# Self attention, two cross attentions and one maximum: three stages of a post-layernorm decoder, re-ordered

## The chip, the cores and the metric

The kernel runs on one core of one Trainium2 chip. A core has a matrix engine (TensorE, PE in the rows), a vector engine (VectorE, DVE), an activation engine (ScalarE, ACT) and a general one (GpSimd, POOL); SyncE (SP) issues the transfers here. The engines run at the same time and keep order through semaphores that the program sets and waits for. The metric is the time of the device for one launch, in microseconds, as the median of several runs.

## The reference

`x` is [32, 56, 128] (32 sequences of 56 tokens, width 128), `ctx` is [32, 1500, 128]. Six sublayers follow each other, each inside `x = layernorm(x + sublayer(x))`. The ones that the change touches are the first, the second and the fifth.

```python
def _L0_attn_ref(x, ...):            # 16 heads of 8, window of 32
    scores = einsum('bhqd,bhkd->bhqk', q, k) * scale + sliding_window_bias(S)
    attn = softmax(scores); out = einsum('bhqk,bhkd->bhqd', attn, v)
    return out.reshape(B, S, D) @ wo.T + bo
def _L0_xattn_ref(k, v, q, ...):     # one head of 128, k = v = ctx
    qp = q @ Wq.T + bq; kp = k @ Wk.T; vp = v @ Wv.T + bv
    return (softmax(qp @ kp.T * scale) @ vp) @ Wo.T + bo
def _L1_xattn_ref(x, context, ...):  # 16 heads of 64, 1500 keys
    q = (_layernorm(x, ln_gamma, ln_beta) @ w_q); k, v = split(context @ w_kv)
    attn = softmax(einsum('bqhd,bkhd->bhqk', q * SCALE, k))
    return (einsum('bhqk,bkhd->bqhd', attn, v) @ w_out + b_out) * tanh(gate)
```

The others are a mixture of experts (top 2 of 8, exact gelu) as the third, a gated state-space layer as the fourth, and a mixture of experts with a shared one (silu) as the sixth.

## The kernel before

Two sequences make a pair: 128 rows on the partitions, 64 for each with 56 in use. There are 16 pairs. Tokens stay on the chip between sublayers, once with rows on the partitions (`x_tok`) and once turned (`x_feat`). Each sublayer is a phase with a block of its own: a program for each engine, written by hand. The order within an engine is the order of the code, and the semaphores between engines are all that ties them.

**PairSteps** drives the first two phases. A step runs every stage once, each on another pair: in self attention project (lag 0), scores 1, transpose 2, attend 3, output 4, norm 5, so six pairs are under way. Each engine's `step(i, s)` asks `pair(i, s, "scores")` and so on for its pair and issues what that stage has for the engine. The body of the loop holds two steps; steps ahead of it fill and steps behind it drain. **Tail** ends each sublayer: VectorE takes the moments of the row sum `r` (L261, L265), GpSimd makes `rstd` of them (L270, L275), VectorE normalises to `xn` (L292), GpSimd copies it to `x_tok`, TensorE turns it, ScalarE stores it in `x_feat` (L349), and where a router follows TensorE makes 8 logits and VectorE copies them (L359).

**Self attention** (`self_attention_phase`, prefix `sa_`). GpSimd expands the keys of a pair so that each head has its own columns (`kexp`, L469, two instructions of 128x896) and adds the output bias to the tokens of a pair (`xbo`). TensorE makes the scores (L510). VectorE adds the window mask (L583, `sm`), takes the maximum of each head (L588), subtracts it (L590), sums after ScalarE's exponential (L597, L599), keeps the masked values (`vexp`, L603), adds projected output and `xbo` (L612, `r`), and keeps the attended values divided by the sum (`on`, L622). The output projection is L549; the attended values stand behind it.

**First cross attention** (`context_attention_phase`, prefix `ca_`). Stages: project 0, scores 1, transpose 2, values 3, output 4, norm 5. Scores fill four banks of PSUM with 375 columns each; one VectorE instruction takes the negated maximum over the 1500 (L907). The probabilities are turned by TensorE (12 blocks, in three parts of four) and copied by VectorE and ScalarE (L915, L939). VectorE also takes the greatest magnitude of the context, one reduction over 128x3000 a step (`ca_tops`, L946), which the second cross attention needs; the next load of `ctxT` into this buffer (L728, on SyncE's queue) waits for it and for the scores. `qp` (L901) is the projected query with bias and scale, L922 makes `r`.

**Second cross attention** (`cross_attention_phase`, prefix `xa_`). The queries of a pair are multiplied ahead with the product of key and query weights (L2072), so the context itself is the key. A pair has 14 units, 7 for each sequence; a unit is 8 queries times 16 heads on 128 rows against 1500 keys, in three banks of 500 columns. Units take banks 0 to 2 and 3 to 5 in turn. For precision queries and context are split in a high and a low part, so TensorE makes three matmuls for each bank: L2087, L2088, L2089. Then, for a unit:

- VectorE takes the maximum in two instructions: L2215 over the first two banks, into a spare column (500) of the second bank; L2219 over that second bank's whole 512 columns from there on, which are that column, eleven filled with a very low number, and the third bank's 500.
- ScalarE takes the exponential over the three banks with its sum (L2333); VectorE sums up and inverts (L2224, L2226).
- ScalarE writes the high part of the probabilities to SBUF (L2349), VectorE the low part, piece by piece (L2234, three instructions). Each of these frees one bank (`h2_ready`) for the unit after the next.
- The probabilities are turned by a transposing DMA, in two units of a pair by TensorE with copies by VectorE (L2240). The matmuls on values (L2112 to L2114) come per group of units.

In a step VectorE's order is: inverse of the unit before, turned copy if any, maximum of this unit, the low part of the unit before. In slots 2 to 5 TensorE also projects (L2072) for the next pair; in slots 7 to 9 it makes the output of the pair before; in 10 to 13 stand the residual, normalise, store and logits of that pair.

## Time and profile before

| what | us |
|---|---|
| median of 3 runs (lowest, highest) | 2001.07 (1999.9, 2002.27) |
| profiled execution: its time, its span | 1998.59, 1996.9 |
| TensorE busy: matmuls, weight loads | 1750.6 (88%), 1266.5 (63%) |
| VectorE, ScalarE, GpSimd busy | 1593.3 (80%), 1186.7 (59%), 830.3 (42%) |
| masked additions L583 of self attention, 16 | starts 28.8 to 141.2 |
| context loads L728 of the first cross attention | issued 181.5 to 317.2 |
| score matmuls L2087 of the second cross attention, 672 | starts 701.6 to 1776.4 |

Durations and stretches come from one profiled execution. The three stages can be told apart in it by their lines. The second cross attention takes more than half of the span, some 1080 us of 1997; each of the other two takes between 110 and 190. Busy shares over the span mix the stages, so a table by stretches is more use.

### The profile page before, as it was taken

To read this page: it belongs to the slowest core of one execution; us is meant where nothing else is said; L and a number is where in the kernel's file an instruction comes from. 1 tells how busy PE (TensorE), PEld (TensorE's weight loads), DVE (VectorE), ACT (ScalarE), POOL (GpSimd) and SP (SyncE) were. 2 spreads that over 40 slices of the span, in tenths; PEclk is the share of its full clock that TensorE was granted. 3 is DMA by queue.
4 is the path that set the end of the run, shared out by engine and by line. 5 is a ranking of instruction groups with operands and counts; after the bars stand their busy time and mean duration, and the time that the engine had idled before them with its cause. 6 is when DMAs were issued, how large, how long until landed. Compare 5 with 4: busy or idle time off the path is not lost. (4 is left out here: it accounts for less than half of the span.)

```text
span 1996.9 us, 34496 instructions
## 1 busy us (share of the span) xinstructions
PE 1750.6 (88%) x10381; PEld 1266.5 (63%) x10381; DVE 1593.3 (80%) x2986; ACT 1186.7 (59%) x1868; POOL 830.3 (42%) x705
## 2 busy tenths in 40 slices
PE   4886888699956379999999999999999999994997
PEld 3554656688842256666667666766666676654886
DVE  3884676678867379988998999899889988966887
ACT  2441332577732167777777777777777777754553
POOL 4660111223342373636364545455454546322333
PEclk9997998699976589999999999999999999997998
DMA  5101775100000079898989888989888998971000
GB/s 192 77 0 62 301 279 233 43 1 0 1 0 0 32 157 206 174 192 178 193 175 192 184 189 178 186 186 182 188 179 191 179 196 173 190 127 72 6 5 10
DMA packets 623534, 264.97 MB, mean 133 GB/s; under 512 B 601565, under 2 KB 605693, under 8 KB 622717
## 3 DMA queue, kind: packets, MB, share of 16 engines
q1 hardware_dynamic: 623468, 264.19, 57.1%
q8 instruction: 31, 0.51, 0.1%
q14 instruction: 35, 0.28, 0.0%
HBM read 112.24 MB, written 0.92 MB: 57 GB/s over the span
## 5 line engine op out<-in xcount | busy, mean ns | idle before, releaser
L2234 DVE SCALAR_TENSOR_TENSOR xa_h<-xa_psum,xa_rinv,xa_h 128x500 f16<-128x500 f32 x672 | 452.5, 729 | 0.7 <-ACT xa_h L2349 0.7
L2333 ACT ACTIVATE xa_psum<-xa_psum,xa_negmax 128x1500 f32<-128x1500 f32 x224 | 332.7, 1485 | 198.0 <-DVE xa_negmax L2219 198.0
L2349 ACT ACTIVATE xa_h<-xa_psum,xa_rinv 128x1000 f16<-128x1000 f32 x448 | 372.2, 883 | 82.5 <-DVE xa_rinv L2226 81.2
L2215 DVE TENSOR_REDUCE xa_psum<-xa_psum 128x1 f32<-128x1000 f32 x224 | 269.5, 1203 | 88.1 <-PE xa_psum L2089 88.1
L2087 PE MATMUL xa_psum<-xa_c_hi,xa_q_hi 128*128 128x500 f32 x672 | 282.9, 421 | 28.5 <-DVE xa_h L2234 18.3
L2112 PE MATMUL xa_psum<-xa_prT,xa_n_hi 128*128 128x512 f16 (+1 forms) x768 | 272.9, 355 | 2.4 <-DMA xa_prT<-xa_h 1.5
L2114 PE MATMUL xa_psum<-xa_prT,xa_n_lo 128*128 128x512 f16 (+1 forms) x768 | 270.7, 352 | 0.0
L2113 PE MATMUL xa_psum<-xa_prT,xa_n_hi 128*128 128x512 f16 (+1 forms) x768 | 270.7, 352 | 0.0
L2088 PE MATMUL xa_psum<-xa_c_lo,xa_q_hi 128*128 128x500 f32 x672 | 262.5, 391 | 0.0
L2089 PE MATMUL xa_psum<-xa_c_hi,xa_q_lo 128*128 128x500 f32 x672 | 262.2, 390 | 0.0
L2219 DVE TENSOR_REDUCE xa_negmax<-xa_psum 128x1 f32<-128x512 f32 x224 | 154.9, 691 | 25.8
L2006 POOL CAST xa_q_hi<-xa_q_full 128x896 fp32r<-128x896 f32 x32 | 29.9, 934 | 347.5 <-PE xa_psum L2089 336.5
L2087 PEld LDWEIGHTS xa_psum<-xa_c_hi,xa_q_hi 128*128 128x128 f32 x672 | 127.4, 190 | 71.9 <-DVE xa_h L2234 31.7
L1406 DVE TENSOR_TENSOR moe_hid_lo<-moe_hid,moe_hid_hi 128x448 fp32r<-128x448 f32 x200 | 127.5, 667 | 31.3 <-ACT moe_hid_hi L1542 26.0
L2089 PEld LDWEIGHTS xa_psum<-xa_c_hi,xa_q_lo 128*128 128x128 f32 x672 | 127.2, 189 | 26.1
L2112 PEld LDWEIGHTS xa_psum<-xa_prT,xa_n_hi 128*128 128x128 f16 x768 | 76.0, 99 | 104.4 <-issue 55.0
L2026 POOL TENSOR_SCALAR xa_ctxP<-xa_ctxP,xa_n_scale 128x1536 f32<-128x1536 f32 x32 | 133.3, 4167 | 17.5 <-DMA xa_ctxP<-in_ctxP 17.5
L2088 PEld LDWEIGHTS xa_psum<-xa_c_lo,xa_q_hi 128*128 128x128 f32 x672 | 128.1, 191 | 11.5
L2114 PEld LDWEIGHTS xa_psum<-xa_prT,xa_n_lo 128*128 128x128 f16 x768 | 75.1, 98 | 70.1
L1253 POOL TENSOR_TENSOR moe_acc<-moe_acc,moe_part 128x448 f32<-128x448 f32 x52 | 63.5, 1222 | 123.2 <-DVE moe_part L1459 65.6
L1538 ACT ACTIVATE moe_hid<-moe_psum,up_bias 128x448 f32<-128x448 f32 x128 | 83.9, 656 | 43.9 <-PE moe_psum L1294 40.0
L2019 POOL TENSOR_TENSOR xa_c_lo<-xa_ctxT,xa_c_hi 128x1500 fp32r<-128x1500 f32 x32 | 107.9, 3372 | 2.6
(303 smaller groups left out, 3613.8 us busy)
## 6 DMA issues: line engine op xcount, KB each, us to landing
ctxN<-in_ctxP SPq DMA_DIRECT2D x16, 1536.0 KB, 9.2
xa_ctxP<-in_ctxP SPq DMA_DIRECT2D x32, 768.0 KB, 4.4
ctxT<-in_ctxT SPq DMA_DIRECT2D x16, 1500.0 KB, 6.3
xa_ctxT<-in_ctxT SPq DMA_DIRECT2D x32, 750.0 KB, 4.9
xa_prT<-xa_h SPq DMA_TRANSPOSE x192, 5.5
up<-in_F_up SPq DMA_DIRECT2D x1, 2048.0 KB, 9.2
down<-in_F_down SPq DMA_DIRECT2D x1, 2048.0 KB, 13.3
gate<-in_F_gate SPq DMA_DIRECT2D x1, 1024.0 KB, 4.8
```

The costliest lines, as they stand in the source:

```text
L2026: pool.tensor_scalar(ctxP[:, :], ctxP[:, :], n_scale[:, :], None, ALU.mult).then_inc(n_scaled, 1)
L2087: nc.tensor.matmul(out, qh, c_hi[:, b, a:z], start=True, stop=False)
L2088: nc.tensor.matmul(out, qh, c_lo[:, b, a:z], start=False, stop=False)
L2089: done = nc.tensor.matmul(out, ql, c_hi[:, b, a:z], start=False, stop=True)
L2112: nc.tensor.matmul(out, nh, ph, start=(kt == 0), stop=False)
L2113: nc.tensor.matmul(out, nh, pl, start=False, stop=False)
L2114: done = nc.tensor.matmul(out, nl, ph, start=False, stop=(kt == KT - 1))
L2215: nc.vector.tensor_reduce(psum[:, bank + 1, W:W + 1], psum[:, bank:bank + 2, 0:W], AX.XY, ALU.max)\
L2219: nc.vector.tensor_reduce(negmax[:, s % 2, :], flat_psum[:, top:top + 512], AX.X, ALU.max, negate=True)\
L2234: nc.vector.scalar_tensor_tensor(h[:, H_SLOT[s], 1, a:z], psum[:, bank + j, 0:W], rinv[:, s % 2, :], h[:, H_SLOT[s], 0, a:z], ALU.mult, AL ...
L2333: nc.scalar.activation(psum[:, bank:bank + 3, 0:W], psum[:, bank:bank + 3, 0:W], ACT.Exp, bias=negmax[:, s % 2, :], accum_out=rs[:, s % 2, ...
L2349: nc.scalar.activation(h[:, H_SLOT[s], 0, a * W:z * W].rearrange("p (a c) -> p a c", c=W), psum[:, bank + a:bank + z, 0:W], ACT.Identity, ...
```

## The change

It has three parts. In **self attention** the bias row is added to all of `x_tok` once at the start, by VectorE, in place of GpSimd's addition for each pair. VectorE sums and inverts ahead of the normalise; the subtraction (L613 of the kernel after) stands behind the masked values, no longer right behind the maximum. GpSimd expands keys ahead of its store. TensorE's turned output and output projection come later in the step, the attended values are cut in two parts around the turned `xn`, and scores go half by half of the heads. ScalarE keeps `oT` later.

In the **first cross attention** the reduction over the context is cut in two (one for each sequence), the first behind the negated maximum, the second at the end of the step; `top_ready` counts halves. `qp` comes ahead of the normalise, the logits have a stage of their own (lag 6), values come in three parts, and TensorE's transposes come ahead of the turned output.

In the **second cross attention** a unit's maximum is one instruction over its three banks, behind all nine matmuls; the spare column, its filling and the semaphore between the two instructions go.

```diff
--- before.py
+++ after.py
@@ -412,7 +412,6 @@
...
-                at = pair(i, s, "attend")
-                if at:
-                    j, p = at
-
-                    pool.wait_ge(t.r_ready, last(j, p + 1, PER))
-                    pool.tensor_tensor(xbo[:, p:p + 1, :], k.x_tok[:, bass.ds(j * PER + p, 1), :],
-                                       k.bo_row0[:, :].unsqueeze(1), ALU.add).then_inc(xbo_ready, 1)
+                at = pair(i, s, "norm")
+                if at:
+                    t.pool_store(pool, *at)
...
+            def attend(j, p, part):
+
+                if part == 0:
+                    pe.wait_ge(prT_kept, this(j, p + 1, PER))
+                    pe.wait_ge(v_kept, this(j, p + 1, PER))
+
+                    pe.wait_ge(o_kept, this(j, p, PER))
+                for hp in range(part * HP // 2, (part + 1) * HP // 2):
+                    for half in range(2):
+                        done = nc.tensor.matmul(psum[half * SP:(half + 1) * SP, 6, hp * 16:(hp + 1) * 16],
+                                                prT[:, p, hp, half * SP:(half + 1) * SP],
+                                                vexp[:, p, half, hp * 16:(hp + 1) * 16], start=True, stop=True)
+                if part:
+                    done.then_inc(o_ready, 1)
+
...
+                at = pair(i, s, "output")
+                if at:
+                    j, p = at
+                    pe.wait_ge(o_kept, this(j, p + 1, PER))
+
+                    pe.wait_ge(t.r_ready, this(j, p, PER))
+                    nc.tensor.transpose(psum[:, 7, 0:128], on[:, p, :], k.ident[:, :]).then_inc(oT_ready, 1)
+                at = pair(i, s, "attend")
+                if at:
+                    attend(*at, 0)
...
+            nc.vector.tensor_tensor(k.x_tok[:, :, :], k.x_tok[:, :, :],
+                                    k.bo_row0[:, :].unsqueeze(1).to_broadcast([128, PAIRS, D]), ALU.add).then_inc(rows_biased, 1)
+            dve.wait_ge(rows_biased, 1)
 
...
-                    dve.wait_ge(xbo_ready, this(j, p + 1, PER))
-                    nc.vector.tensor_tensor(t.r[:, p, :], psum[:, 7, 128:256], xbo[:, p, :], ALU.add)\
-                        .then_inc(t.r_ready, 1)
+                    nc.vector.tensor_tensor(t.r[:, p:p + 1, :], psum[:, 7, 128:256].unsqueeze(1),
+                                            k.x_tok[:, bass.ds(j * PER + p, 1), :], ALU.add).then_inc(t.r_ready, 1)
                     t.vector_moments(dve, j, p)
...
-    steps = PairSteps(project=0, scores=1, transpose=2, values=3, output=4, norm=5)
+    steps = PairSteps(project=0, scores=1, transpose=2, values=3, output=4, norm=5, logits=6)
...
+                sp.sem_inc(issuing, 1)
+                sp.wait_ge(top_ready, last(i, 2 * p + 2, 2 * PER))
...
-                for kt in range(part * KT // 2, (part + 1) * KT // 2):
+                for kt in range(part * KT // 3, (part + 1) * KT // 3):
...
-                    pe.wait_ge(t.logits_kept, n(i, s, 6))
...
+                at = pair(i, s, "logits")
+                if at:
+                    pe.wait_ge(qp_kept, n(i, s, 0))
+                    pe.wait_ge(t.r_ready, n(i, s, 5))
+                    pe.wait_ge(t.feat_stored, n(i, s, 6))
+                    t.tensor_logits(pe, *at, psum[:, 7, 384:384 + E])
...
+                at = pair(i, s, "values")
+                if at:
+                    j, p = at
...
-                    pe.wait_ge(qp_kept, n(i, s, 0))
+                    pe.wait_ge(t.logits_kept, n(i, s, 6))
...
+                    values(at[1], 1)
...
-                    values(at[1], 1).then_inc(pv_ready, 1)
+                    values(at[1], 2).then_inc(pv_ready, 1)
...
-                at = pair(i, s, "norm")
-                if at:
-                    pe.wait_ge(t.feat_stored, n(i, s, 5))
-                    pe.wait_ge(t.r_ready, n(i, s, 4))
-                    pe.wait_ge(qk_kept, n(i, s, 0))
-                    t.tensor_logits(pe, *at, psum[:, 7, 384:384 + E])
...
+            def top(i, s, half):
+
+                at = pair(i, s, "scores")
+                if at:
+                    j, p = at
+                    if half == 0:
+                        dve.wait_ge(ctxT_loaded[p], (j + 1) * 16)
+                    nc.vector.tensor_reduce(tops[:, bass.ds(j * 2 * PER + 2 * p + half, 1)], ctxT[:, p, half, :], AX.X,
+                                            ALU.max, apply_absolute_value=True).then_inc(top_ready, 1)
+
             def step(i, s):
...
+                top(i, s, 0)
...
-                    dve.wait_ge(ctxT_loaded[p], (j + 1) * 16)
-                    nc.vector.tensor_reduce(tops[:, bass.ds(j * PER + p, 1)], ctxT[:, p, :, :], AX.XY, ALU.max,
-                                            apply_absolute_value=True).then_inc(top_ready, 1)
+                top(i, s, 1)
...
+                at = pair(i, s, "project")
+                if at:
...
-                    if j:
-                        done.then_inc(scores_ready, 1)
+                done.then_inc(scores_ready, 1)
...
             def maximum(i, s):
                 bank = 3 * (s % 2)
-                top = (bank + 1) * 512 + W
-                dve.wait_ge(scores_ready, this(i, 2 * s + 1, 2 * NU))
-                nc.vector.tensor_reduce(psum[:, bank + 1, W:W + 1], psum[:, bank:bank + 2, 0:W], AX.XY, ALU.max)\
-                    .then_inc(two_ready, 1)
-                dve.wait_ge(two_ready, this(i, s + 1, NU))
-                dve.wait_ge(scores_ready, this(i, 2 * s + 2, 2 * NU))
-                nc.vector.tensor_reduce(negmax[:, s % 2, :], flat_psum[:, top:top + 512], AX.X, ALU.max, negate=True)\
+                dve.wait_ge(scores_ready, this(i, s + 1, NU))
+                nc.vector.tensor_reduce(negmax[:, s % 2, :], psum[:, bank:bank + 3, 0:W], AX.XY, ALU.max, negate=True)\
                     .then_inc(max_ready, 1)
 
```

VectorE in self attention, one step of the filling: `sa_sm` are the scores, `sa_mx` their maxima, `sa_rs` and `sa_rinv` sum and inverse, `sa_r` the row sum. Before:

```order
L292 TENSOR_SCALAR sa_xn<-sa_r,sa_mean_var,sa_rstd 128x128
L583 TENSOR_TENSOR sa_sm<-sa_psum,window_mask 128x896
L588 TENSOR_REDUCE sa_mx<-sa_sm 128x16
L590 TENSOR_TENSOR sa_sm<-sa_sm,sa_mx 128x896
L597 TENSOR_REDUCE sa_rs<-sa_pr 128x16
L599 RECIPROCAL sa_rinv<-sa_rs 128x16
L603 TENSOR_TENSOR sa_vexp<-sa_psum,value_mask 112x256
L612 TENSOR_TENSOR sa_r<-sa_psum,sa_xbo 128x128
L261 BN_STATS sa_moments<-sa_r 128x6
L265 BN_AGGR sa_mean_var<-sa_moments 128x2
L622 TENSOR_TENSOR sa_on<-sa_psum,sa_rinv 128x128
```

and after:

```order
L581 TENSOR_REDUCE sa_rs<-sa_pr 128x16
L583 RECIPROCAL sa_rinv<-sa_rs 128x16
L292 TENSOR_SCALAR sa_xn<-sa_r,sa_mean_var,sa_rstd 128x128
L593 TENSOR_TENSOR sa_sm<-sa_psum,window_mask 128x896
L598 TENSOR_REDUCE sa_mx<-sa_sm 128x16
L605 TENSOR_TENSOR sa_vexp<-sa_psum,value_mask 112x256
L613 TENSOR_TENSOR sa_sm<-sa_sm,sa_mx 128x896
L620 TENSOR_TENSOR sa_r<-sa_psum,x_tok 128x128
L261 BN_STATS sa_moments<-sa_r 128x6
L265 BN_AGGR sa_mean_var<-sa_moments 128x2
L630 TENSOR_TENSOR sa_on<-sa_psum,sa_rinv 128x128
```

Sum and reciprocal moved from behind the subtraction to the head of the step, and the subtraction (L590, now L613) past the masked values.

VectorE in the first cross attention, one step: `ca_tops` is the reduction over the context, `ca_qp` the projected query. Before:

```order
L292 TENSOR_SCALAR ca_xn<-ca_r,ca_mean_var,ca_rstd 128x128
L901 TENSOR_SCALAR ca_qp<-ca_psum,bq0x 128x112
L907 TENSOR_REDUCE ca_negmax<-ca_psum 128x1
L915 COPY ca_prT<-ca_psum 128x512
L922 SCALAR_TENSOR_TENSOR ca_r<-ca_psum,ca_rinv,ca_xb 128x128
L261 BN_STATS ca_moments<-ca_r 128x6
L265 BN_AGGR ca_mean_var<-ca_moments 128x2
L931 RECIPROCAL ca_rinv<-ca_rs 128x1
L359 COPY logits<-ca_psum 128x8
L939 COPY ca_prT<-ca_psum 128x512
L946 TENSOR_REDUCE ca_tops<-ctxT 128x1
```

and after, with the last reduction of the step before in the first row (in the loop the logits copy stands behind L292):

```order
L910 TENSOR_REDUCE ca_tops<-ctxT 128x1
L920 TENSOR_SCALAR ca_qp<-ca_psum,bq0x 128x112
L292 TENSOR_SCALAR ca_xn<-ca_r,ca_mean_var,ca_rstd 128x128
L934 COPY ca_prT<-ca_psum 128x512
L940 TENSOR_REDUCE ca_negmax<-ca_psum 128x1
L910 TENSOR_REDUCE ca_tops<-ctxT 128x1
L948 SCALAR_TENSOR_TENSOR ca_r<-ca_psum,ca_rinv,ca_xb 128x128
L261 BN_STATS ca_moments<-ca_r 128x6
L265 BN_AGGR ca_mean_var<-ca_moments 128x2
L957 RECIPROCAL ca_rinv<-ca_rs 128x1
L959 COPY ca_prT<-ca_psum 128x512
L910 TENSOR_REDUCE ca_tops<-ctxT 128x1
```

The copy of the turned probabilities now comes ahead of the negated maximum, and the reduction (L946, now L910) stands twice, once between the negated maximum and `ca_r` and once at the end.

VectorE in the second cross attention, from the turned copy of one unit to its low part. Before:

```order
L2239 REGISTER_ALU
L2240 COPY xa_prT<-xa_psum 128x4x2x128
L2214 REGISTER_ALU
L2215 TENSOR_REDUCE xa_psum<-xa_psum 128x1
L2217 REGISTER_ALU
L2218 REGISTER_ALU
L2219 TENSOR_REDUCE xa_negmax<-xa_psum 128x1
L2234 SCALAR_TENSOR_TENSOR xa_h<-xa_psum,xa_rinv,xa_h 128x500 x3
```

and after:

```order
L2244 REGISTER_ALU
L2245 COPY xa_prT<-xa_psum 128x4x2x128
L2223 REGISTER_ALU
L2224 TENSOR_REDUCE xa_negmax<-xa_psum 128x1
L2238 REGISTER_ALU
L2239 SCALAR_TENSOR_TENSOR xa_h<-xa_psum,xa_rinv,xa_h 128x500 x2
L2238 REGISTER_ALU
L2239 SCALAR_TENSOR_TENSOR xa_h<-xa_psum,xa_rinv,xa_h 128x500
```

One reduction stands where two stood; nothing else changed places.

## Rows read from the trace of the kernel before

**Rows 1.** Stretches: us, busy of PE (count), PEld, DVE, ACT, POOL; PEclk, DMA, GB/s

```profile
46.67:141.22 94.55, 80.88 (x723) 57.32 (x724) 77.12 (x133) 39.96 (x83) 65.13 (x71) 0.93 0.13 55
216.88:313.80 96.92, 81.25 (x775) 56.81 (x774) 68.57 (x101) 28.15 (x72) 13.24 (x37) 1.00 0.75 291
766.80:1716.30 949.50, 939.76 (x5391) 650.50 (x5391) 855.83 (x1527) 709.78 (x981) 482.57 (x253) 1.00 0.89 185
```

**Rows 2.** Self attention, VectorE in time: start us, us, work [wait]; then L590's durations

```profile
93.85 0.35 DVE L292 TENSOR_SCALAR sa_xn<-sa_r,sa_mean_var,sa_rstd 128x128 f32<-128x128 f32 x1 [0.85 <-POOL sa_rstd L275]
...
100.96 0.34 DVE L292 TENSOR_SCALAR sa_xn<-sa_r,sa_mean_var,sa_rstd 128x128 f32<-128x128 f32 x1 [0.72 <-POOL sa_rstd L275]
...
L590 DVE TENSOR_TENSOR sa_sm<-sa_sm,sa_mx x16: 1091/1235/2637, 31.1 to 143.5; 128x896 f32<-128x896 f32 x16
```

**Rows 3.** Self attention, TensorE and GpSimd in time

```profile
89.09 0.46 PE L549 MATMUL sa_psum<-woT,sa_oT 128*128 128x128 f32 x2 [0.81 <-ACT x_feat L349]
...
101.80 3.34 POOL L469 TENSOR_TENSOR sa_kexp<-sa_kf,head_mask 128x896 f32<-128x896 f32 x2
```

**Rows 4.** First cross attention, around the turn of one step, in time

```profile
259.90 3.27 DVE L946 TENSOR_REDUCE ca_tops<-ctxT 128x3000 f32 x1
...
263.43 0.37 SPq L728 DMA_DIRECT2D ctxT<-in_ctxT  x1
...
263.58 1.71 DVE L907 TENSOR_REDUCE ca_negmax<-ca_psum 128x1 f32<-128x1500 f32 x1
...
263.72 0.33 PE L825 MATMUL ca_psum<-ident,ca_o_tok 128*128 128x128 f32 x1 [1.06 <-DVE ca_qp L901]
...
265.21 0.68 DVE L915 COPY ca_prT<-ca_psum 128x512 f32<-128x512 f32 x1
...
268.33 0.49 PE L867 MATMUL ca_psum<-value_out,ca_oT 128*128 128x128 f32 x2
...
268.86 0.35 DVE L922 SCALAR_TENSOR_TENSOR ca_r<-ca_psum,ca_rinv,ca_xb 128x128 f32<-128x128 f32 x1 [2.97 <-PE ca_psum L867]
...
270.42 0.47 PE L805 MATMUL ca_psum<-x_feat,wqT0x 128*128 x2 [0.75 <-DVE logits L359]
```

**Rows 5.** Second cross attention, one unit of the first pair, in time

```profile
725.09 0.49 PE L2087 MATMUL xa_psum<-xa_c_hi,xa_q_hi 128*128 128x500 f32 x1 [1.11 <-DVE xa_h L2234]
...
726.56 0.39 PE L2087 MATMUL xa_psum<-xa_c_hi,xa_q_hi 128*128 128x500 f32 x1
...
726.76 1.21 DVE L2215 TENSOR_REDUCE xa_psum<-xa_psum 128x1 f32<-128x1000 f32 x1 [0.17 <-PE xa_psum L2089]
...
727.24 1.04 PE L2072 MATMUL xa_psum<-x_feat,key_query 128*128 128x112 f32 x8
...
728.61 2.02 DVE L2234 SCALAR_TENSOR_TENSOR xa_h<-xa_psum,xa_rinv,xa_h 128x500 f16<-128x500 f32 x3
...
729.39 0.49 PE L2087 MATMUL xa_psum<-xa_c_hi,xa_q_hi 128*128 128x500 f32 x1 [1.11 <-DVE xa_h L2234]
```

**Rows 6.** The same phase, a steady pair: first score matmuls of five units

```profile
1195.91 0.48 PE L2087 MATMUL xa_psum<-xa_c_hi,xa_q_hi 128*128 128x500 f32 x1
...
1200.82 0.48 PE L2087 MATMUL xa_psum<-xa_c_hi,xa_q_hi 128*128 128x500 f32 x1
...
1205.33 0.47 PE L2087 MATMUL xa_psum<-xa_c_hi,xa_q_hi 128*128 128x500 f32 x1
...
1210.65 0.48 PE L2087 MATMUL xa_psum<-xa_c_hi,xa_q_hi 128*128 128x500 f32 x1
...
1215.76 0.47 PE L2087 MATMUL xa_psum<-xa_c_hi,xa_q_hi 128*128 128x500 f32 x1
```

**Rows 7.** The page's groups: busy, mean ns; idle before them, releaser

```profile
L2087 PE MATMUL xa_psum<-xa_c_hi,xa_q_hi 128*128 128x500 f32 x672 | 282.9, 421 | 28.5 <-DVE xa_h L2234 18.3
...
L2219 DVE TENSOR_REDUCE xa_negmax<-xa_psum 128x1 f32<-128x512 f32 x224 | 154.9, 691 | 25.8
```

**Rows 8.** Loads of the turned context (L728), from issue to landing

```profile
DMA to landing us min/median/max: 6.0/6.2/7.7
```

More of the change, by code:

```diff
@@ L507, in step @@
                     pe.wait_ge(masked, this(j, p, PER))
-                    for half in range(2):
-                        for hh in range(2):
+                    for hh in range(2):
+                        for half in range(2):
                             done = nc.tensor.matmul(psum[half * SP:(half + 1) * SP, hh, 0:8 * S], qs[:, p, half, :],
@@ L542, in step @@
                     t.tensor_transpose(pe, *at, psum[:, 7, 256:384])
+                at = pair(i, s, "attend")
+                if at:
+                    attend(*at, 1)
                 at = pair(i, s, "output")
@@ L550, in step @@
                         .then_inc(y_ready, 1)
-                at = pair(i, s, "attend")
-                if at:
-                    j, p = at
-                    pe.wait_ge(prT_kept, this(j, p + 1, PER))
-                    pe.wait_ge(v_kept, this(j, p + 1, PER))
-                    pe.wait_ge(o_kept, this(j, p, PER))
-                    for half in range(2):
-                        for hp in range(HP):
-                            done = nc.tensor.matmul(psum[half * SP:(half + 1) * SP, 6, hp * 16:(hp + 1) * 16],
-                                                    prT[:, p, hp, half * SP:(half + 1) * SP],
-                                                    vexp[:, p, half, hp * 16:(hp + 1) * 16], start=True, stop=True)
-                    done.then_inc(o_ready, 1)
             steps.run(pe, step)
@@ L670, in step @@
                                          psum[0:2 * S, 4:6, :], ACT.Copy).then_inc(prT_kept, 1)
+                at = pair(i, s, "output")
+                if at:
+                    j, p = at
+                    act.wait_ge(oT_ready, this(j, p + 1, PER))
+                    act.wait_ge(y_ready, last(j, p + 1, PER))
+                    nc.scalar.activation(oT[:, p, :], psum[:, 7, 0:128], ACT.Identity, bias=k.bv0[:, :])\
+                        .then_inc(oT_kept, 1)
                 at = pair(i, s, "norm")
@@ L916, in step @@
                         .then_inc(even_kept, 1)
+                at = pair(i, s, "scores")
+                if at:
+                    j, p = at
+                    dve.wait_ge(scores_ready, this(j, p + 1, PER))
+                    nc.vector.tensor_reduce(negmax[:, p, :], psum[:, 0:4, 0:Q4], AX.XY, ALU.max, negate=True)\
+                        .then_inc(max_ready, 1)
+                top(i, s, 0)
                 at = pair(i, s, "output")
@@ L940, in step @@
                         .then_inc(even_kept, 1)
[L941 to L947 removed]
+                top(i, s, 1)
             steps.run(dve, step)
[L950 removed]
+            dve.wait_ge(top_ready, last(PAIRS // PER, 2 * PER, 2 * PER))
             nc.vector.tensor_reduce(k.ctx_max[:, :], tops[:, :], AX.X, ALU.max).then_inc(ctx_max_ready, 1)
```

123 lines of the change are left out of this document (47 added, 76 removed).

## The prediction

> **What bounds the kernel now.** The change touches three stages, so I read the table of stretches first [rows 1]. Self attention, between the masked additions of the fourth and the sixteenth pair, runs 12 steps in 94.55 us, 7.88 each. The first cross attention runs 9 steps in 96.92 us, 10.77 each. The second cross attention runs 14 pairs of 14 units in 949.5 us: 67.82 a pair, 4.84 a unit. TensorE is busy 86%, 84% and 99%, VectorE 82%, 71% and 90%. Busy shares don't say who waits for whom, so I then read each stage in order of time.
>
> Self attention: from one normalise to the next 7.11 us pass on VectorE, 0.72 of them waiting for the rstd of GpSimd [rows 2], since normalise stands first in the step and the moments it needs were made just before. VectorE's own work is thus 6.39. TensorE idles 0.81 of the same step before the output projection, which waits for x_feat [rows 3]: 6.30. Some steps are longer than 7.1: the subtraction takes 1.09 us at the least and 2.64 at the most [rows 2] while GpSimd works 3.34 of each step on the expanded keys [rows 3].
>
> First cross attention: the reduction over the context (3.27 us) is the last VectorE instruction of a step; behind it stand normalise and qp, and TensorE waits 1.06 us for qp before its transposition. It waits 0.75 more, at the start of a step, for the logits copy [rows 4]. So TensorE needs 10.77 - 1.06 - 0.75 = 8.96 us.
>
> Second cross attention: TensorE does the nine score matmuls of a unit, then values and what else the unit has. The next unit's scores wait for VectorE's low part, which frees their banks, and which stands behind the maximum. This loop is seen bare in the first pair [rows 5]: scores at 725.09, first maximum at 726.76 (after six matmuls, +1.67), low part at 728.61 (+1.85), next scores at 729.39 (+0.78): 4.30 us, with TensorE idle for 1.11. In the steady pairs TensorE has 4.91 of work in a unit with a projection, 5.32 and 5.11 with outputs, 4.51 with a turn [rows 6]. So this loop is hidden nearly everywhere, but by 0.2 to 0.6 us only.
>
> **The second cross attention after.** VectorE now issues one reduction of 128x1500 where it issued 1000 and 512. The same shape is in the first cross attention: 1.71 us, and the next instruction starts 1.63 after its start [rows 4]. Against the 1.85 of the two, VectorE saves 0.22 a unit. But the reduction can't start after six matmuls any more. Nine are issued in 2.15 us, and the last three of them in 0.68 (726.56 to 727.24) [rows 5], so it starts at +1.67 + 0.68 = +2.35. The loop becomes 2.35 + 1.63 + 0.78 = 4.76, and 0.46 longer where it was bare.
>
> What lies beside other work: the four projection units (4.91) and the three output units (5.32, 5.11 and, not shown, as much again) stay TensorE's, 35.2 us. The other seven units of a pair took 67.82 - 35.2 = 32.6, and take 7 x 4.76 = 33.3 after, plus 0.07 for the unit where the logits copy stands between maximum and low part: +0.8 a pair, +11 for 14 pairs. In the first pair thirteen units run on the bare loop or near it, and in the last pair, where projections are missing, seven do: about 20 x 0.35 = +7. Sum: +18. ScalarE, the transposes by DMA and GpSimd have slack: the exponential moves 0.4 later, and the high part waits for it, but the low part that reads it is a maximum further on. Bounds for the unknown, the reduction's length: from 1.71 (its row) up to 1.90, the two old durations together (1.21 and 0.69) [rows 7]; that gives a loop of 4.95 and +35. Down: if part of the third group's wait were hidden, 4.60, about +5.
>
> **The first cross attention after.** On VectorE qp now stands first, normalise second, the logits copy third, the reduction is cut in two halves, one behind the negated maximum (where VectorE waited for the output matmul) and one at the end; logits are a stage later, so TensorE no longer ends its step on them. Each half is about 1.7 (a 128x1500 row). Both waits go. What is late next: (a) the new step's first matmul needs r: the output matmul starts at 268.33 and r at 268.86 [rows 4], r lasts 0.35, so 1.1 us lie between the output matmul and the next step, of which TensorE fills, as I count, 1.0 with the last four transposes; (b) logits, now right behind the scores, need qp, and qp waits for the second half reduction, which ends some 2.8 us into the step, while scores end at 2.9: about 0.3 of wait. 8.96 + 0.3 = 9.25 a step. From the fifth step to the sixteenth's scores 11 steps gain 1.5: -16.5; filling is bound by context loads, issued only behind a reduction as before, and draining sheds 1.6 of the reduction once: -1. Sum -17. Bounds: 8.96 and no wait, -21; context loads, below, -12.
>
> **Self attention after.** Sum and reciprocal now stand ahead of normalise, 1.3 us of work that covers the 0.72; the output projection stands behind attend, which covers the 0.81; the bias row is added once for all pairs, so GpSimd loses an addition a step. Neither engine waits then, and VectorE's 6.39 is the longer one: 6.45 with TensorE beside it. 12 x (7.88 - 6.45) = -17. Filling and draining: the sum now waits for the whole exponential, which nothing covers before outputs exist, an estimated +1 (it works on as many elements as the subtraction, 1.09), and the single addition over 128x2048 runs before any key is expanded, about 2.3 us (1.09 for 896) in a time when VectorE had nothing to do, and may hold GpSimd's first keys back, +0.5. Drain steps lose an attend's wait, -1. Sum -16.5. The reordering inside scores and attend I take at 0; it cannot cost more than the idle it leaves.
>
> **A rule weighed.** The subtraction is not slower by a steady factor; it is 1.09 or up to one key expansion longer [rows 2]. The Trainium skill, SBUF, "Who interferes with whom", says that a VectorE instruction with two SBUF inputs and a GpSimd instruction that reads SBUF shut each other out for a whole instruction. The trace agrees, with 2.64 against 1.09. By that rule the new placement matters: the keys of a step end, by my count, 0.05 us before the later subtraction starts. If it starts first, 1.5 us a step can be lost again; that is the third rival.
>
> **Sum.** +18 - 17 - 16.5 = -15.5 against the profiled execution: span 1996.9, its time 1998.6. That is 1983. The median of the runs shown, 2001.1, lies 2.5 above this execution, so I predict 1985.5.
>
> **The rivals.**
> First: VectorE bounds the second cross attention, and a shorter maximum is a plain gain. For it: busy 90%, the tightest of the three stages, in which TensorE's score matmuls waited 18.3 us for the low part [rows 7]. The Trainium skill, VectorE: DVE Perf Modes, section on the TRN2 errata, says that each instruction pays a fixed cost and that few large ones are better. By rows: all these waits of TensorE go, 18.3 us, and in total 2001 - 33 - 18 = 1950. Against it: VectorE is idle before the maximum in the bare loop and TensorE waits all the same [rows 5]. Chance 0.05.
> Second, slower: the bare loop grows past 4.91. Then the four projection units pay as well, eleven a pair, and each further 0.1 costs 1.1 x 14 + 2 = 17 us. The gains of 33.5 are eaten when the loop reaches about 4.93, that is when the reduction lasts 1.88, not 1.71. At 2.0 it is 5.05 and the total about 2018. For it: three banks of 500 in one instruction were never timed here; against it: the 1.71 row spans four banks. Chance 0.07.
> Third: subtraction and key expansion meet in every second step, self attention keeps 7.1 or so: -8 in place of -16.5, total 1994. Chance 0.13.
> Fourth: context loads bind the first cross attention. A load lands 6.0 to 7.7 us after its issue [rows 8], which is 0.26 behind the reduction's end [rows 4]; at a step of 9.25 about 6.5 us are left for it. If loads take 7.5, steps are 9.7: 5 us less gain, 1990. Chance 0.12.
> Fifth: the reordering changes neither stage much because each wait removed is replaced by a neighbour's, 2003 with the second cross attention's +18 and half the gains. Chance 0.05.
>
> **Numbers.** Forecast 1977 to 1993, chance 0.58. The range that holds 8 in 10 goes from 1972 (all small bounds good) to 1998, where rivals three and four together end. A measurement of this kernel tells 0.2%, 4 us, from nothing. Faster: forecast, first, fourth, most of the third: 0.85. Same, 1997 to 2005: 0.08. Slower: 0.07.
>
> **What would show it.** In the second cross attention a reduction of 1.71, the bare loop at 4.76, pairs at 68.6, TensorE's idle before the first score matmul up, VectorE's busy time down. In the first, steps of 9.25 and no wait for qp before the transposition. In self attention steps of 6.45, a normalise without wait, subtractions of 1.09. Wrong would be: pairs under 67.8 or over 70, steps over 10 or over 7.

## The result, and the profile after

| | before | after |
|---|---|---|
| median, us (lowest, highest; runs) | 2002.12 (1999.9, 2006.05; 8) | 1992.47 (1988.81, 1996.72; 8) |
| profiled execution's span | 1996.9 | 1988.5 |
| VectorE busy | 1593.3 | 1568.3 |

The ratio is 0.9948, with a 95% interval from 0.9934 to 0.9961: 10.4 us less, between 7.8 and 13.2. The forecast was 15.5 less. Faster, clear of the noise though only by half a percent, and two thirds of the size. The median of 1992.47 lies inside the range of 1977 to 1993 by half a microsecond only.

I compare when the same events start in the two traces:

| event | before | after | difference |
|---|---|---|---|
| 4th masked addition, self attention | 46.67 | 46.77 | +0.1 |
| 16th masked addition | 141.22 | 129.96 | -11.3 |
| 1st negated maximum, first cross attention | 176.47 | 162.26 | -14.2 |
| 16th negated maximum | 327.82 | 301.04 | -26.8 |
| first score matmul, second cross attention | 701.6 | 670.6 | -31.0 |
| last of them | 1776.4 | 1767.6 | -8.8 |

So some 31 us were won before the second cross attention began, and 22 were given back in it. The table of stretches of the kernel after (us, busy of PE, PEld, DVE, ACT, POOL, PEclk, DMA share, GB/s) answers to [rows 1]; the stretches run between the same events, but the last holds fourteen pairs within 1 us:

```profile
46.77:129.96 83.19, 68.39 (x719) 46.55 (x717) 78.98 (x133) 38.57 (x82) 50.06 (x59) 1.00 0.15 63
207.20:291.91 84.71, 82.15 (x778) 56.00 (x776) 69.99 (x109) 28.76 (x73) 12.98 (x36) 1.00 0.86 331
758.00:1718.60 960.60, 949.87 (x5379) 648.71 (x5378) 829.41 (x1330) 707.65 (x978) 481.79 (x252) 1.00 0.88 183
```

Self attention's twelve steps take 6.93 each (7.88 before), nine steps of the first cross attention 9.41 (10.77), a pair of the second 68.61 (67.82). In self attention VectorE is now busy 95%, and TensorE's granted clock is 1.00 where it was 0.93 (1.00 is 2.4 GHz, and it falls to 0.50, 1.2 GHz, for some us at a time).

**Self attention.** One step in order of time, VectorE and GpSimd, which answers to [rows 2, 3]:

```profile
86.48 1.08 DVE L581 TENSOR_REDUCE sa_rs<-sa_pr 128x16 f32<-128x896 f32 x1
...
87.06 3.33 POOL L465 TENSOR_TENSOR sa_kexp<-sa_kf,head_mask 128x896 f32<-128x896 f32 x2
...
87.88 0.95 DVE L292 TENSOR_SCALAR sa_xn<-sa_r,sa_mean_var,sa_rstd 128x128 f32<-128x128 f32 x1
...
88.75 1.08 DVE L593 TENSOR_TENSOR sa_sm<-sa_psum,window_mask 128x896 f32<-128x896 f32 x1
```

The durations (lowest, median, highest, in ns) of the normalise and the subtraction:

```profile
L292 DVE TENSOR_SCALAR sa_xn<-sa_r,sa_mean_var,sa_rstd x16: 288/954/1200, 52.5 to 151.5; 128x128 f32<-128x128 f32 x16
...
L613 DVE TENSOR_TENSOR sa_sm<-sa_sm,sa_mx x16: 1081/1082/1091, 31.8 to 132.4; 128x896 f32<-128x896 f32 x16
```

VectorE doesn't wait for the rstd in front of the normalise any more, as forecast, and the subtraction is at its 1.08. But the normalise, 0.35 before, has a median of 0.95; in the steady steps it is 0.95 and 1.14 in turn. The masked addition behind it starts at 88.75: that is 87.06 plus 1.69, the end of the first of GpSimd's two key instructions.

**First cross attention.** Around the turn of a step, answering to [rows 4]:

```profile
249.68 0.47 PE L814 MATMUL ca_psum<-x_feat,wqT0x 128*128 x2 [0.23 <-DVE ca_r L948]
...
250.72 1.70 DVE L910 TENSOR_REDUCE ca_tops<-ctxT 128x1500 f32 x1
252.34 0.32 DVE L920 TENSOR_SCALAR ca_qp<-ca_psum,bq0x 128x112 f32<-128x112 f32 x1
...
252.67 0.37 SPq L739 DMA_DIRECT2D ctxT<-in_ctxT  x1
252.75 0.39 PE L355 MATMUL ca_psum<-router,ca_xnT 128*128 128x8 f32 x2
...
259.28 2.75 PE L825 MATMUL ca_psum<-ctxT,ca_qk 128*64 128x375 f32 x16
```

TensorE doesn't wait for qp here, where it waited 1.06, and it waits 0.23 for `ca_r` ahead of the projection, where it waited 0.75 for the logits copy. The next load is issued 0.25 behind the end of the second half (250.72 plus 1.70).

**Second cross attention.** One unit of the first pair, answering to [rows 5]:

```profile
696.89 0.49 PE L2098 MATMUL xa_psum<-xa_c_hi,xa_q_hi 128*128 128x500 f32 x1 [1.58 <-DVE xa_h L2239]
...
699.05 1.04 PE L2083 MATMUL xa_psum<-x_feat,key_query 128*128 128x112 f32 x8
699.25 1.72 DVE L2224 TENSOR_REDUCE xa_negmax<-xa_psum 128x1 f32<-128x1500 f32 x1 [0.86 <-PE xa_psum L2100]
...
701.54 1.37 DVE L2239 SCALAR_TENSOR_TENSOR xa_h<-xa_psum,xa_rinv,xa_h 128x500 f16<-128x500 f32 x2
701.67 0.50 PE L2098 MATMUL xa_psum<-xa_c_hi,xa_q_hi 128*128 128x500 f32 x1 [1.58 <-DVE xa_h L2239]
```

The reduction lasts 1.72, it starts 2.36 after the first score matmul, and the unit takes 4.78. VectorE has less work and waits more; TensorE waits 1.58 where it waited 1.11.

### The profile page after: what moved, and what is told of

It is laid out like the page before. It is cut to its first block and busy times, and to the rows that moved or that the text cites. A ratio compares the mean times of both kernels' runs of the same rounds, so it can differ in the third digit from the quotient of the medians.

```text
span 1988.5 us, 34045 instructions
## 1 busy us (share of the span) xinstructions
PE 1749.0 (88%) x10381; PEld 1249.8 (63%) x10381; DVE 1568.3 (79%) x2777; ACT 1184.4 (60%) x1868; POOL 810.5 (41%) x689
## 5 line engine op out<-in xcount | busy, mean ns | idle before, releaser
L2224 DVE TENSOR_REDUCE xa_negmax<-xa_psum 128x1 f32<-128x1500 f32 x224 | 385.5, 1721 | 166.9 <-PE xa_psum L2100 166.9
L2122 PEld LDWEIGHTS xa_psum<-xa_prT,xa_n_hi 128*128 128x128 f16 x768 | 76.0, 99 | 104.4 <-issue 55.1
L2123 PEld LDWEIGHTS xa_psum<-xa_prT,xa_n_hi 128*128 128x128 f16 x768 | 75.6, 98 | 49.1
```

The source lines that it names most:

```text
L2122: nc.tensor.matmul(out, nh, ph, start=(kt == 0), stop=False)
L2123: nc.tensor.matmul(out, nh, pl, start=False, stop=False)
L2224: nc.vector.tensor_reduce(negmax[:, s % 2, :], psum[:, bank:bank + 3, 0:W], AX.XY, ALU.max, negate=True)\
```

## The experiments

Unless said otherwise a run's kernel is timed against the kernel before on the same chip; a difference in us is the ratio's times 2001. Intervals are 95%.

**The three parts, one at a time.** The kernels take whole functions from one kernel or the other, so no edit is shown.

> The kernel before with the single maximum of the second cross attention and nothing else of the change. Theory (the loop scores, maximum, low part, next scores has become 4.76 us, and only units in which TensorE has less than that pay): +21.6 us as read from the starts of the maxima in the trace after (6.6 in the first pair, 12.0 in fourteen steady pairs, 3.0 in the last), so about 2023 in place of 2001, a maximum of 1.72 us and a bare loop of 4.76. Rival (part of the 21.6 is due to the stages ahead, which end earlier in another state of clock or queues): 10 to 17 us.

Measured: 2021.08, ratio 1.0104 (1.0085 to 1.0123), +20.8 us. Bare units are 4.75 to 4.79. The theory stands; the 17 of the rival lies at the edge of the interval (17.0 to 24.6), but in this run's profile the stage alone, from its first maximum to its last, is 1093.2 where it was 1072.0, so 21.2 of it are the stage's own.

> The kernel after with the maximum of before in two instructions: both reorderings without the new maximum. Theory: the gains of the two stages stand by themselves, -30 us against before (1971), and the bare loop is 4.30 again. Rival (the earlier stages' gain is partly given back in the second cross attention whatever its maximum, since the first loads and the first clock dip move with it): only -20 to -25.

Measured: 1967.70, ratio 0.9847 (0.9825 to 0.9869), -30.6. Bare units are 4.30. The rival falls.

> The kernel before with the new order of self attention alone. Theory: -14 us (to 1987): steady steps of 7.03 in place of 7.87, the drain 3 shorter, the start 0.7 longer. Rival (part of the shorter drain and the early start of the first cross attention belongs to that phase's own new order): -11, as far as the last masked addition shows.

Measured: 1985.65, ratio 0.9926 (0.9908 to 0.9945), -14.8. The theory's size; the rival's -11 lies at the edge of the interval.

> The kernel before with the new order of the first cross attention alone. Theory: -15.5 (to 1985.5): steady steps of 9.38 in place of 10.74, eleven of them 14.7, the drain 3 less, the filling 1.8 to 2 longer since its steps wait for loads of the turned context. Rival (the loads wait only because self attention ends earlier and the context is not yet there): the filling is no longer than before and the gain is -17 to -18.

Measured: 1985.26, ratio 0.9931 (0.9911 to 0.9952), -13.8. Theory and rival both lie in the interval (-17.8 to -9.6). The first five maxima are 10.38, 7.47, 8.60 and 8.54 apart, against 6.77, 7.27, 8.97 and 10.65 before: 1.3 longer. But this filling differs from one execution to the next without any edit: with the order of before it takes 33.7 in the profile of the kernel before and 37.7 in that of the run with the new maximum alone, and with the new order 33.8, 35.4 and 36.3 in three profiles of kernels that are the same up to there (both orders with the maximum of before, the kernel after, the late start below). So the profiles can't tell whether the new order fills more slowly, and theory and rival both stay open.

The three add up to -7.8, the whole is -10.4, within the intervals the same. Parts that touch separate stages add up here.

**Why the new maximum costs.** VectorE's work of before, but with the start of after:

```diff
-                dve.wait_ge(scores_ready, this(i, 2 * s + 1, 2 * NU))
+                dve.wait_ge(scores_ready, this(i, 2 * s + 2, 2 * NU))
```

> Both reorderings with the maximum of before in two instructions, but the first of them waits for all nine matmuls too, as the single maximum does. Theory (the loop's length is what counts, and the late start, not the length of the reduction, is the price): loop 2.35 + 1.85 + 0.78 = 4.98; seven units of a steady pair at 4.98 in place of 32.6 us together give 2.3, the four projection units 0.07 each 0.3, so 36 for fourteen pairs, and 0.68 on 20 bare units 13.6: about +50 over 1967.7, 2018. Rival (VectorE's work sets these units): its work is the same as before, so no more than +5.

Measured: 2027.48, one run, +60 over the run with both orders and the maximum of before (2002 was the kernel before there, 2000 beside that run, so 2 us of it may be the chip's), where +50 was expected. In the profiles 53 of the 60 are in this stage: from its first maximum to its last 1125.8 pass where 1072.4 did. The bare units:

```profile
695.57 1.21 DVE L2229 TENSOR_REDUCE xa_psum<-xa_psum 128x1 f32<-128x1000 f32 x1 [0.84 <-PE xa_psum L2103]
696.82 0.69 DVE L2233 TENSOR_REDUCE xa_negmax<-xa_psum 128x1 f32<-128x512 f32 x1
697.42 2.02 DVE L2248 SCALAR_TENSOR_TENSOR xa_h<-xa_psum,xa_rinv,xa_h 128x500 f16<-128x500 f32 x3
...
698.21 0.50 PE L2101 MATMUL xa_psum<-xa_c_hi,xa_q_hi 128*128 128x500 f32 x1 [1.79 <-DVE xa_h L2248]
...
700.55 1.21 DVE L2229 TENSOR_REDUCE xa_psum<-xa_psum 128x1 f32<-128x1000 f32 x1 [0.85 <-PE xa_psum L2103]
```

From 695.57 to 700.55 is 4.98, as worked out. With no more work for VectorE the kernel loses far more than the change did: the start behind all nine matmuls is the price, and the single instruction gives back 0.22 of its 0.68. The rival falls.

**Why the normalise is three times as long.** First GpSimd's instructions are halved:

```diff
                     for half in range(2):
-                        done = pool.tensor_tensor(kexp[:, p, half, :, :],
-                                                  kf[:, p, half, :].unsqueeze(1).to_broadcast([128, H0, S]),
+                        for a in range(0, H0, H0 // 2):
+                            done = pool.tensor_tensor(kexp[:, p, half, a:a + H0 // 2, :],
+                                                      kf[:, p, half, :].unsqueeze(1).to_broadcast([128, H0 // 2, S]),
...
```

> Both reorderings with the maximum of before (as in the run of both orders without the new maximum, 1967.7), and GpSimd's key expansion in four instructions of 128x448 in place of two of 128x896. Theory A (VectorE's normalise has to wait until the GpSimd instruction that is running ends, for its whole length): the instruction that is in the way is half as long, so the normalise falls from a median of 0.95 to 0.34 to 0.8, the self attention steps from 7.03 to 6.4 to 6.9, the whole 2 to 6 us less. Rival B (the normalise is longer because it waits for something else, such as a semaphore of the turned xn or the rstd): 0.95 stays and the step is 7.03 or, by the fixed cost of two more GpSimd instructions, longer.

Measured: 1965.84, ratio 0.9813 (0.9792 to 0.9834). The durations of the normalise and of the keys, and then three stretches of 20 us (columns as above):

```profile
L292 DVE TENSOR_SCALAR sa_xn<-sa_r,sa_mean_var,sa_rstd x16: 289/390/1101, 52.9 to 146.5; 128x128 f32<-128x128 f32 x16
...
L465 POOL TENSOR_TENSOR sa_kexp<-sa_kf,head_mask x64: 931/936/1154, 22.4 to 122.0; 128x448 f32<-128x448 f32 x64
```

```profile
60.00:80.00 20.00, 18.57 (x178) 11.99 (x176) 18.88 (x34) 9.53 (x22) 15.46 (x22) 0.91 0.01 2
80.00:100.00 20.00, 17.98 (x173) 11.56 (x172) 18.83 (x33) 9.15 (x21) 15.46 (x22) 0.91 0.00 0
100.00:120.00 20.00, 18.75 (x183) 12.19 (x182) 18.91 (x34) 9.78 (x21) 13.80 (x21) 0.91 0.00 0
```

The normalise falls to a median of 0.39 and B falls. But the steps now alternate, 6.28 and 7.28, and the median hides that the normalise does so too: 0.39 in the short steps, 1.07 to 1.10 in the long ones. TensorE's clock, 1.00 in these stretches of the kernel after, is 0.91. In a long step (in order of time) the scores, 1.72 at full clock, take 2.90, and the normalise is 1.10:

```profile
96.03 2.90 PE L518 MATMUL sa_psum<-sa_kexp,sa_qs 128*64 128x448 f32 x8
...
99.37 1.10 DVE L292 TENSOR_SCALAR sa_xn<-sa_r,sa_mean_var,sa_rstd 128x128 f32<-128x128 f32 x1
```

The clock doesn't make the long steps, though. The step from 79.55 on takes 7.27 as well, with its scores at full clock and the stretched normalise:

```profile
82.83 1.72 PE L518 MATMUL sa_psum<-sa_kexp,sa_qs 128*64 128x448 f32 x8
...
85.81 1.09 DVE L292 TENSOR_SCALAR sa_xn<-sa_r,sa_mean_var,sa_rstd 128x128 f32<-128x128 f32 x1
```

This normalise starts 0.1 before the first key instruction ends (84.99 plus 0.94) and lasts to the end of the second, so halving the instruction shortens the wait in every second step only. The twelve steps save 3.9 us. The total is not clearly below that of the run without this edit.

The second run moves GpSimd's store ahead of its keys, so that keys can't start before the normalise has ended:

```diff
             def step(i, s):
+                at = pair(i, s, "norm")
+                if at:
+                    t.pool_store(pool, *at)
                 at = pair(i, s, "project")
```

> Both reorderings with the maximum of before, but GpSimd does its store (which waits for the normalise) ahead of the key expansion, as in the kernel before. Theory A (the two engines shut each other out for whole instructions): the normalise is back at 0.34, but the keys now run over the subtraction, which has two inputs in SBUF: it rises from 1.08 to between 1.6 and 2.6 in most steps, and the steps are 7.0 or longer, up to 7.9. Rival B (the normalise waits for something of its own): it keeps about 0.95 and the subtraction 1.08.

Measured: 1974.34, one run. Most steps are 7.6 to 7.8, the mean is 7.5.

```profile
L292 DVE TENSOR_SCALAR sa_xn<-sa_r,sa_mean_var,sa_rstd x16: 289/346/348, 52.3 to 155.2; 128x128 f32<-128x128 f32 x16
...
L613 DVE TENSOR_TENSOR sa_sm<-sa_sm,sa_mx x16: 1081/2376/2432, 31.6 to 138.7; 128x896 f32<-128x896 f32 x16
```

The normalise is never over 0.35, and the subtraction has taken its place with a median of 2.38. A holds in both directions: what meets a key instruction waits for its end, and the order only chooses which. The two wait differently: the normalise ends with the key instruction, the subtraction 0.94 behind it (85.26 plus 2.41 is 87.67, the key instruction ends at 86.73).

The third takes the normalise from VectorE:

```diff
+                    nc.scalar.activation(t.xn[:, p, :], t.r[:, p, :], ACT.Identity, bias=minus_mean[:, p, :],
+                                         scale=t.rstd[:, p, :]).then_inc(t.xn_ready, 1)
...
-                    t.vector_normalise(dve, *at)
```

> Both reorderings with the maximum of before, and self attention's normalise on ScalarE as scale and bias (GpSimd makes -mean x rstd in two more small instructions). VectorE then has no instruction left that a key expansion meets, and 0.34 less work. Theory A: VectorE's step is 7.03 - 0.95 = 6.1 of work; TensorE had 5.8 busy with 1.2 idle in the old step, so 6.1 to 6.5 a step, twelve of them 6 to 11 us, 1957 to 1962 in place of 1967.7, and no VectorE instruction of the stage is longer than its own lowest. Rival C (the chain normalise, turned xn, x_feat, projection, keys sets the step, and VectorE's stretched normalise was only slack): 6.9 to 7.1, no gain.

Measured: 1968.51, ratio 0.9829 (0.9812 to 0.9845), the same as without the edit. Most steps are 6.7 to 7.4. Theory A said too much, and of rival C the "no gain" came true: the keys now start later, behind two more GpSimd instructions, and run over the subtraction.

```profile
L622 DVE TENSOR_TENSOR sa_sm<-sa_sm,sa_mx x16: 1081/1586/1911, 31.7 to 130.5; 128x896 f32<-128x896 f32 x16
```

Both edits together:

> Both reorderings with the maximum of before, the self attention normalise on ScalarE and the key expansion in four instructions. In the run with ScalarE's normalise the keys started later, so that the subtraction was the one shut out (median 1.59 in place of 1.08). Theory A: with half as long a GpSimd instruction the subtraction falls under 1.3, and steps go from 6.8 to 6.3 to 6.6 unless the clock of TensorE falls more often: 1962 to 1966. Rival F (TensorE's chain and its clock now set the step, as the alternation of 6.28 and 7.28 with four key instructions suggests): 6.7 to 6.9, no gain over 1965.8 to 1968.5.

Measured: 1968.94, ratio 0.9837 (0.9809 to 0.9864). The subtraction is back at a median of 1.08 (1.24 at most), and still the steps are between 6.4 and 8.6, with no gain in total: A falls, and F's account fits. The trace separates the two things that F names. TensorE's clock fell three times between 57 and 85 us, and the four steps there are 7.5 to 8.6. In the last six it is 1.00 throughout, and they still take 6.7 on average:

```profile
85.12:125.47 40.35, 35.05 (x367) 24.14 (x366) 35.03 (x61) 22.36 (x48) 33.91 (x54) 1.00 0.00 0
```

```profile
106.97 0.48 ACT L688 ACTIVATE sa_xn<-sa_r,sa_minus_mean,sa_rstd 128x128 f32<-128x128 f32 x1
107.36 0.36 ACT L696 ACTIVATE sa_oT<-sa_psum,bv 128x128 f32<-128x128 f32 x1
...
107.94 0.32 PE L332 MATMUL sa_psum<-ident,sa_xn 128*128 128x128 f32 x1 [0.81 <-ACT sa_oT L696]
```

TensorE waits 0.63 to 0.84 in each of these steps for ScalarE's `oT`, which now stands behind the normalise; with the normalise on VectorE the wait there was 0.25 to 0.43. So the move put 0.48 of work into the chain that TensorE waits for. That this wait alone holds the step at 6.7 is not shown.

**Which edit carries the first cross attention.** The halves are undone:

```diff
-                    nc.vector.tensor_reduce(tops[:, bass.ds(j * 2 * PER + 2 * p + half, 1)], ctxT[:, p, half, :], AX.X,
+                    if half == 0:
+                        return
+                    nc.vector.tensor_reduce(tops[:, bass.ds(j * PER + p, 1)], ctxT[:, p, :, :], AX.XY,
```

> Both reorderings with the maximum of before, but the first cross attention's reduction over the context in one instruction of 128x3000 at the end of VectorE's step, as before, with all other orders of the kernel after. Theory D (the halves carry the gain of this stage, since qp must wait for the reduction in either order): qp comes 1.6 us later, TensorE waits for it ahead of the logits by as much, steps 10.6 to 10.9 in place of 9.38, +13 to +16 over 1967.7. Rival E (the moved qp and logits carry it): 9.7 or less a step, +4 at most.

Measured: 1991.09, one run, +23 over 1967.7 where +13 to +16 was expected; steps of 10.93 and two of 12.4 and 13.0. In the profiles eleven steps account for 17 of it, and the filling, where one interval is 13.0, for 4.5. The wait for qp in a steady step:

```profile
249.86 3.27 DVE L912 TENSOR_REDUCE ca_tops<-ctxT 128x3000 f32 x1
...
253.04 0.33 DVE L922 TENSOR_SCALAR ca_qp<-ca_psum,bq0x 128x112 f32<-128x112 f32 x1
...
253.61 0.38 PE L355 MATMUL ca_psum<-router,ca_xnT 128*128 128x8 f32 x2 [1.74 <-DVE ca_qp L922]
```

The halves alone, on the kernel before, with the rest of its order kept:

```diff
                         .then_inc(even_kept, 1)
+                at = pair(i, s, "scores")
+                if at:
+                    top(*at, 0)
...
-                    nc.vector.tensor_reduce(tops[:, bass.ds(j * PER + p, 1)], ctxT[:, p, :, :], AX.XY, ALU.max,
-                                            apply_absolute_value=True).then_inc(top_ready, 1)
+                    top(j, p, 1)
```

> The kernel before with the first cross attention's reduction cut in two halves, one behind VectorE's first copy of the turned probabilities (where VectorE waited 2.97 us for the output matmul), one at the end; no other change. Theory D: the 1.06 that TensorE waited for qp goes, the 0.75 for the logits copy stays: steps of 9.7 in place of 10.74, about -11 (1990). Rival E (halving alone frees nothing, since normalise and qp still stand behind the second half and the logits copy binds the step): 10.5 or longer, 0 to -3.

Measured: 1985.86, one run, 15 below the kernel before where 11 was expected, and as low as with the whole new order of this stage (1985.26 on another chip). Steps of 9.67 where 9.7 was worked out, since TensorE no longer waits for qp; the wait for the logits copy is still there:

```profile
249.67 1.71 DVE L897 TENSOR_REDUCE ca_tops<-ctxT 128x1500 f32 x1
...
251.55 0.33 DVE L910 TENSOR_SCALAR ca_qp<-ca_psum,bq0x 128x112 f32<-128x112 f32 x1
...
252.48 0.33 PE L828 MATMUL ca_psum<-ident,ca_o_tok 128*128 128x128 f32 x1
...
258.96 0.47 PE L808 MATMUL ca_psum<-x_feat,wqT0x 128*128 x2 [0.58 <-DVE logits L359]
```

The new order of everything else takes the step from 9.67 to 9.38, some 3 us over eleven steps, which the times of the two kernels don't show, and without the halves (10.93) it is worse than the order of before (10.74). D holds, E falls, and the halves are nearly all of the gain.

## Why the prediction was right, and where it was off

**The second cross attention.** The bare loop was forecast at 4.76 with a reduction of 1.71; 4.75 to 4.78 with 1.72 were measured, and pairs of 68.61 for 68.6. The mechanism (a later start outweighs a shorter instruction, and only units in which TensorE has less than the loop pay) was shown by the late start alone. The sum was +18 and +20.8 was measured. The trace of the kernel after has +12.1 in the fourteen pairs (11 forecast), +6.6 in the first pair and +3.0 in the last (7 forecast for both). Two units of the first pair make the difference: the second took 6.56 where it was 5.48, and the seventh 6.29 where it was 4.62, when TensorE's clock fell to half after a wait of 2.09.

```profile
706.53 0.47 PE L2098 MATMUL xa_psum<-xa_c_hi,xa_q_hi 128*128 128x500 f32 x1 [2.09 <-DVE xa_h L2239]
...
707.56 0.62 PE L2098 MATMUL xa_psum<-xa_c_hi,xa_q_hi 128*128 128x500 f32 x1
...
710.44 0.38 PE L2123 MATMUL xa_psum<-xa_prT,xa_n_hi 128*128 128x512 f16 x1
```

The other eleven intervals of that pair are 0.35 longer each, just as in the sum. The term for bare units had no price for a clock that falls while TensorE waits. The length of the wait doesn't tell all: in the run with the late start the clock fell after a wait of 1.79, and the units at 698 and 703 had waited as long and kept it.

One bound of the sum was too kind. By its own terms a loop of 4.95 costs about +43, not +35: 0.19 more on the seven units of fourteen pairs and on 20 bare ones, and 0.04 on the projection units. The gains of 33.5 would be gone at a loop of about 4.89, a reduction of 1.84. The late start bears this out: at a loop of 4.98 its stage lost 53.

**The first cross attention.** Steps of 9.25 were forecast, 9.38 to 9.41 measured, the waits for qp and the logits copy went. The term for the steps was somewhat too large: the eleven intervals from the fifth maximum to the sixteenth took 117.7 before and 103.3 after, 14.3 less, where 16.5 was forecast. From there to the second cross attention the trace is 4.2 shorter, where -1 stood; other profiles with the new order put this between nothing and 5. The filling, which I took to be bound by loads as before, at no change, is 1.8 longer in this trace (7.48, 9.49, 8.01 and 10.46 between maxima), which is less than fillings of one order differ by. The third pair's scores waited for a load of the turned context:

```profile
173.57 4.43 PE L825 MATMUL ca_psum<-ctxT,ca_qk 128*64 128x375 f32 x16 [2.73 <-DMA ctxT<-in_ctxT]
```

In sum the trace gives -16.8 for -17 (-16.5 and -1 make -17.5, to be exact), so the errors of the terms cancel in it by luck; the part alone gives -13.8, with -17 inside its interval. My text put the gain down to four edits together and didn't say which; the halves are it.

**Self attention.** Here a step failed: "subtractions of 1.09" and "steps of 6.45". The subtraction was right. The step is 7.03, because the sum took VectorE's work as 6.39 with a normalise of 0.35 [rows 2], and in its new place the normalise meets the key expansion and lasts 0.95 to 1.2. The third rival had the mechanism and its price, but looked only at the subtraction. By the Trainium skill, SBUF, "Who interferes with whom", a `tensor_scalar` too can take the port pair that VectorE shares with GpSimd, in the mode that uses both read ports; the trace agrees, with 0.95 beside a key instruction and 0.35 without one. That rule stands next to the one that the prediction draws on. The forecast was -16.5 and -14.8 was measured, although most steps kept 0.6 more than forecast: twelve steps gave 11.4 instead of 17. Two other terms made up for it, by luck: the filling up to the fourth masked addition cost 0.1 where 1.5 stood, and the way from the last masked addition to the first maximum of the next stage became 3 shorter where 1 stood. Why the end of the stage became shorter stays open.

TensorE's clock, 0.93 before and 1.00 after, is not what the new order gains. The run with the new order of self attention alone has the same steps, 7.04, at a clock of 0.94:

```profile
46.49:129.72 83.23, 72.72 (x719) 48.07 (x717) 79.02 (x133) 38.62 (x82) 50.16 (x59) 0.94 0.15 64
```

In the order of before the four steps in which the scores took 2.9 to 3.3 in place of 1.73 lasted 8.0 to 8.6, two with a subtraction of 2.6 lasted 8.6 to 8.7, and most others 7.1 to 7.4. I read this as a clock that cost time there, while in the new order, with VectorE busy throughout, a delay of TensorE no longer shows in the step.

Nothing of the first rival (VectorE bounds) or the second (a reduction near 1.9) came true. What is true of the first is the length, one instruction of 1.72 in place of 1.21 and 0.69; the time went into the later start. The total was 5 us off. The parts timed alone all err to the same side, +20.8 for +18, -13.8 for -17 and -14.8 for -16.5, but each by less than its interval; by the trace the second cross attention (+22.2) and self attention (-14.2) are off and the first cross attention is not.

**A version that beats both** is at hand: both orders with the maximum in two instructions, 1967.7, 1.5% below the kernel before. With the keys in four instructions the ratio is 0.9813, lowest of all; the two intervals overlap.

## What to carry to other kernels

An instruction that runs on half of its input before the rest is there may be worth more than a shorter one that must wait for all of it: count from the producer's first instruction to the point where its buffer is free. When a long instruction stands where another engine waits, cut it in two and put one half where its own engine idles. And when instructions move, look at what each of them now runs beside, the shortest too: which one a neighbour's long instruction holds up is a matter of order. Before a few us in one profile are put down to an edit, look for a second execution of the same code: here the filling of one stage differed by 4 us without any edit.

## What the runs showed of the hardware

A VectorE `tensor_scalar` of 128x128 from SBUF to SBUF, 0.35 us, lasted until the end of a GpSimd `tensor_tensor` that it met: 0.95 and 1.14 in turn with instructions of 1.69, 0.39 and 1.10 in turn with ones of 0.94, where the 1.10 reached from the end of one over the whole next. A `tensor_tensor` with both inputs in SBUF, 1.08, ended 0.94 behind the key instruction that it met and rose to a median of 2.38. The reductions of 128x896 (1.07 to 1.09) never changed. A reduction of 128x1500 from three banks of PSUM takes 1.72, from four banks 1.71. The same normalise on ScalarE, 128x128 with scale and bias, takes 0.48. TensorE's clock fell to half in the first pair of the second cross attention after a wait of 2.09 (kernel after) and one of 1.79 (late start), while the units in front, with waits of 1.58 and 1.79, kept it. In self attention it is 1.00 in one execution and 0.94 in another of the same order, with the same steps.
